# Attention with layer norm beside a quantised FFN on one core: keys and probabilities turned by DMA, context taken out in 16 blocks, queries turned in their own tile

## What is computed

```python
xn = (x - mean) / sqrt(var + 1e-5)
# attention over the HEADS of one token: 32 heads of 32 numbers
q, k, v = (xn @ W.T + b).reshape(B, S, 32, 32)     # for Wq, Wk, Wv
scores = einsum('bshd,bsgd->bshg', q, k) / sqrt(32)
scores = where(scores > 0.001, scores, -inf)
out = einsum('bshg,bsgd->bshd', softmax(scores), v)
attn = out.reshape(B, S, 1024) @ Wo.T + bo
# FFN with weights q * scale, one scale for 128 inputs
ffn = (silu(xn @ Wg.T) * (xn @ Wu.T)) @ Wd.T
return x + attn + ffn
```

## Time and profile before

| | |
|---|---|
| median of 3 runs | 2207.91 us (2207.07 to 2210.4) |
| profiled execution, its own time | 2210.67 us |
| its span | 2208.9 us |
| TensorE busy | 2100.9 us, 95% |
| VectorE busy | 1664.8 us, 75% |
| ScalarE busy | 1374.9 us, 62% |
| GpSimd busy | 1361.2 us, 62% |
| mean granted TensorE clock | 0.993 of full speed |

### The profile page before, as it was taken

The page is one execution under the profiler, slowest core; times in us unless marked ns, Lnnn a source line. Parts: engine busy times, 40 slices in busy tenths (PEclk is TensorE's granted clock), DMA queues, the critical chain, the costliest instruction groups (busy, mean ns, idle before and its releaser), DMA issues. The chain is left out here.

```text
span 2208.9 us, 39955 instructions
## 1 busy us (share of the span) xinstructions
PE 2100.9 (95%) x12032; PEld 1041.6 (47%) x12032; DVE 1664.8 (75%) x1904; ACT 1374.9 (62%) x2353; POOL 1361.2 (62%) x785
## 2 busy tenths in 40 slices
PE   7999999999999899989999999999999999999996
PEld 5555555555555554433444444444444444444444
DVE  5576667766676631049989989998998999999896
ACT  4687787887878743124565566656656665665653
POOL 1345435444445401005888888888888888888886
PEclk9999999999999999999999999999999999999998
DMA  8001000001001133412212211221221122122118
GB/s 286 30 30 40 36 28 34 32 28 47 28 28 38 68 105 113 160 34 67 57 47 52 70 44 47 66 57 47 60 64 43 47 66 57 47 66 57 43 25 309
DMA packets 156187, 144.08 MB, mean 65 GB/s; under 512 B 101488, under 2 KB 130160, under 8 KB 156144
## 3 DMA queue, kind: packets, MB, share of 16 engines
q1 hardware_dynamic: 156144, 143.50, 21.4%
HBM read 96.29 MB, written 25.17 MB: 55 GB/s over the span
## 5 line engine op out<-in xcount | busy, mean ns | idle before, releaser
L681 PE MATMUL banks<-xt,lower 128*128 128x512 f16 x3584 | 861.7, 379 | 29.9 <-ACT lower L935 16.3
L1253 POOL TENSOR_TENSOR acc<-acc,lower 128x1024 f32<-128x1024 f32 x327 | 772.1, 2365 | 176.2 <-ACT lower L962 176.2
L962 ACT ACTIVATE lower<-banks,down_scale 128x512 f32<-128x512 f32 x654 | 413.7, 683 | 356.5 <-PE banks L706 261.5
L1135 DVE SCALAR_TENSOR_TENSOR lower<-banks,gate_scale,lower 128x1024 f32<-128x1024 f32 x392 | 479.2, 1277 | 139.4 <-PE banks L681 133.5
L681 PEld LDWEIGHTS banks<-xt,lower 128*128 128x128 f16 x3584 | 337.4, 98 | 486.6 <-DVE lower L1135 80.2
L528 PE MATMUL banks<-wt,xt_tile 128*128 128x512 f16 x2304 | 552.7, 379 | 8.0 <-issue 4.1
L1135 DVE SCALAR_TENSOR_TENSOR lower<-banks,up_scale,lower 128x1024 f32<-128x1024 f32 x392 | 479.5, 1278 | 51.1 <-PE banks L681 44.9
L706 PE MATMUL banks<-lower 128*128 (+1 forms) x1792 | 459.8, 381 | 4.6 <-DMA lower<-lower 4.4
L1210 POOL TENSOR_TENSOR stacks<-unit,stacks 128x512 f16<-128x512 f32 x192 | 225.4, 1198 | 385.3 <-ACT stacks L807 385.3
L528 PEld LDWEIGHTS banks<-wt,xt_tile 128*128 (+1 forms) x2304 | 212.3, 98 | 205.0 <-issue 7.5
L706 PEld LDWEIGHTS banks<-lower 128*128 (+1 forms) x1792 | 175.7, 98 | 217.7 <-issue 18.5
(11 more groups left out here) (65 smaller groups left out, 1572.1 us busy)
## 6 DMA issues: line engine op xcount, KB each, us to landing
lower<-in_L_ffn_gate_q_dram SPq DMA_DIRECT2D x28, 512.0 KB, 3.7
lower<-in_L_ffn_up_q_dram SPq DMA_DIRECT2D x28, 512.0 KB, 4.4
lower<-in_L_ffn_down_q_dram SPq DMA_DIRECT2D x28, 512.0 KB, 3.9
x_tile<-in_L_attn_x_dram SPq DMA_DIRECT2D x16, 512.0 KB, 3.6
xt_scratch<-xt_tile SPq DMA_DIRECT2D x16, 512.0 KB, 2.7
ctx_scratch<-ctx_parts SPq DMA_DIRECT2D x16, 512.0 KB, 2.8
lower<-ctx_scratch SPq DMA_DIRECT2D x4, 2048.0 KB, 9.0
xt<-xt_scratch SPq DMA_DIRECT2D x4, 2048.0 KB, 16.3
```

The costliest lines, as they stand in the source:

```text
L681: last = mm(psum[:, 2 * (slot % 3) + c, :], gu_t[:, mat, g, :], xt[:, (2 * half + c) * CT:(2 * half + c + 1) * CT, part, g, :], start=(par ...
L962: run(down_tmp[:, buffer, c * BANK:(c + 1) * BANK], psum[:, 6 + c, :], ACT.Copy, scale=scale)\
L1135: v.scalar_tensor_tensor(out=acc_of[:, half, :], in0=gu_pair(slot % 3), scalar=scale[:, :, :].rearrange("p t k -> p (t k)")[:, bass.ds(t * ...
L1253: g.tensor_tensor(acc[:, half, ho, :], acc[:, half, ho, :], down_tmp[:, buffer, :], ALU.add).then_inc(down_added, 1)
```

## The change

Keys: SP issues one DMA transpose of 1 MB in a round, from `stacks` to `turned`, once the key units have both parts and the last scores of the tile before are made. Probabilities: four DMA transposes of 256 KB in a round, one for each eight groups, once their low part is made. TensorE keeps eight batches in a round: four of queries, now of tile i in round i (R0 to R3, steps 11 to 14), and four of values of tile i - 1 (T4 to T7, steps 4 to 7). Scores stand at steps 0 to 3, value products at 17 to 20. A group now holds tokens that lie 32 apart, so that a diagonal block of the context holds 32 neighbouring tokens. The score matmul reads the turned keys with strides, (x, r) for a fixed group g, out of [x, r, g], and its output has the order (h, r). ScalarE takes a block of the context out of PSUM straight into the high part, VectorE subtracts for the low part, 16 instructions each in a round; the reordering over partitions is left to four DMA stores of 128 KB, with runs of 1 KB. The context for the output units has runs of 32 columns in place of 128.

The core of the diff ("..." marks what is left out):

```diff
-        STEPS = [["T0"], ["T1"], ["T2"], ["T3"], ["T4"], ["T5"], ["T6", "T7"], ["S0"], ["S1"], ["S2"],
-                 ["S3"], ["T8"], ["T9"], ["T10"], ["T11"], ["X"], [], [], [], ["T12"], ["T13", "V0"],
-                 ["T14", "V1"], ["T15", "V2"], ["V3"]]
+        STEPS = [["S0"], ["S1"], ["S2"], ["S3"], ["T4"], ["T5"], ["T6"], ["T7"], [], ["X"], [], ["R0"], ["R1"],
+                 ["R2"], ["R3"], [], [], ["V0"], ["V1"], ["V2"], ["V3"], [], [], []]
-        STATS_AT, ROOT_AT, NORM_AT, SHIFT_AT, EXP_AT, MASK_AT, DIVIDE_AT, P_AT = 6, 8, 9, 10, 11, 12, 13, 15
-        CONTEXT_AT = 2
+        STATS_AT, ROOT_AT, NORM_AT, SHIFT_AT, EXP_AT, MASK_AT, DIVIDE_AT, P_AT = 0, 2, 2, 3, 4, 5, 6, 8
...
+        def block_of(k, r):
+            src = pair(v_pair(k)).rearrange("p (g r a b) -> p r b a g", r=TG, a=KT, b=TG)
+            return src[r * DH:(r + 1) * DH, r, :, :, :]
+        def context_block(k, r, part):
+            return ctx_parts[r * DH:(r + 1) * DH, :, part, :, 8 * k:8 * k + 8]
+        k_turns = turned[:, K, :].rearrange("p (x r g) -> p x r g", r=TG, g=GROUPS)
...
             def scores(j, k):
                 if k == 0:
+                    pe.wait_ge(batch_out[0], j * 4 + 2)
+                    pe.wait_ge(batch_out[1], j * 4 + 2)
+                    pe.wait_ge(k_turned, j * 16 + 16)
+                    wait_pos(pe, ctx_lo, j * 4)
                 elif k >= 2:
                     pe.wait_ge(s_out, j * 4 + (k - 1))
                 for n in range(8):
                     at = (8 * k + n) * P
                     last = mm(pair(s_pair(k))[:, n * P:(n + 1) * P], turned[:, Q, at:at + P],
-                              turned[:, K, at:at + P], start=True, stop=True)
+                              k_turns[:, :, :, 8 * k + n], start=True, stop=True)
...
             def head_products(j, k):
...
-                    pe.wait_ge(pv_out[0], j * 4 + (k - 1))
-                    pe.wait_ge(pv_out[1], j * 4 + (k - 1))
-                pe.wait_ge(batch_out[k % 2], j * 8 + (6 + k // 2 + 1))
+                    pe.wait_ge(ctx_lo, j * 4 + (k - 1))
+                pe.wait_ge(p_turned[k], j * 16 + 16)
...
+            def first_tile():
+                opening(weights, lambda: turn_x(0), first_quarter, lambda: None, lambda: turn_x(1))
+                for m in range(4):
+                    batch(0, m)
...
+            def head_products_hi(j, k):
                 act.wait_ge(pv_done, j * 4 + (k + 1))
                 if k == 0:
+                    wait_pos(act, ctx_stored, j * 64)
+                for r in range(TG):
+                    last = run(context_block(k, r, HI), block_of(k, r), ACT.Copy)
+                last.then_inc(ctx_hi, 1)
...
+            def head_products_lo(j, k):
+                dve.wait_ge(ctx_hi, j * 4 + (k + 1))
+                for r in range(TG):
+                    last = v.tensor_tensor(context_block(k, r, LO), block_of(k, r), context_block(k, r, HI),
+                                           ALU.subtract)
+                last.then_inc(ctx_lo, 1)
...
+            def turn_k(i):
+                if isinstance(i, int) and i == 0:
+                    sp.wait_ge(w_turned, 3 * KT)
+                sp.wait_ge(unit_lo, i * 6 + (2 * K + 2))
+                anchor(sp)
+                wait_pos(sp, s_done, i * 4)
+                anchor(sp)
+                sp.dma_start_transpose(turned[:, K, :].rearrange("p (x t) -> p x t", t=P), stacks[:, K, :, :].rearrange("p x c -> p (x c)"))\
+                    .then_inc(k_turned, 16)
+            def turn_probs(j, q):
+                sp.wait_ge(p_lo, j * 4 + (q + 1))
+                if q == 0:
+                    anchor(sp)
+                    wait_pos(sp, pv_done, j * 4)
+                anchor(sp)
+                at = slice(8 * q, 8 * q + 8)
+                sp.dma_start_transpose(probs_t[:, :].rearrange("p (g c) -> p g c", c=P)[:, at, :],
+                                       p_stack[:, at, :, :].rearrange("p g n h -> p (g n h)"))\
+                    .then_inc(p_turned[q], 16)
...
             def tile_2(i):
                 if not isinstance(i, int) or i + 1 < TT:
                     load_x(i + 1)
-                    store_xt(i + 1)
+                if not isinstance(i, int) or i > 1:
+                    store_context(i - 2)
                 if not projects(i):
                     for n in range(2, KT):
                         load_wo(n)
+                for q in range(4):
+                    turn_probs(i - 1, q)
+                if not isinstance(i, int) or i + 1 < TT:
+                    store_xt(i + 1)
+                if projects(i):
+                    turn_k(i)
...
                     load_wo(0)
                     load_wo(1)
-                    sp.wait_ge(ctx_stored, 16 * 2 * CT)
+                    sp.wait_ge(ctx_stored, 64 * 2 * CT)
                     load_context(0)
-                store_context(i - 1)
```

More of the change, by code:

```diff
@@ L165, in build @@
         unit_lo = sem("unit_lo")
+        k_turned = sem("k_turned")
+        p_turned = [sem(f"p_turned{k}") for k in range(4)]
         batch_done = sem("batch_done")
@@ L534, in batch @@
             def batch(j, m):
[L536 to L541, removed]
+                mat = batch_matrix(m)
+                if m % 4 == 0:
+                    pe.wait_ge(unit_lo, j * 6 + (2 * mat + 2))
+                wait_pos(pe, batch_out[m % 2], j * 4 + m // 2)
                 for n in range(8):
-                    x = 8 * (m % 4) + n
-                    src = stacks[:, m // 4, x, :] if m < 12 else p_stack[:, x, :, :].rearrange("p a b -> p (a b)")
-                    last = turn(batch_bank(m)[:, n * P:(n + 1) * P], src, ident16[:])
+                    last = turn(batch_bank(m)[:, n * P:(n + 1) * P], stacks[:, mat, 8 * (m % 4) + n, :], ident16[:])
                 last.then_inc(batch_done, 1)
@@ L644, in tile_2 @@
                             turn_x(i + 1)
+                        elif kind == "R":
+                            batch(i, n)
                         elif kind == "T":
@@ L650, in tile_2 @@
                             head_products(i - 1, n)
-            walk(pe, lambda: opening(weights, lambda: turn_x(0), first_quarter, lambda: None,
-                             lambda: turn_x(1)), tile_2)
+            def first_tile():
+                opening(weights, lambda: turn_x(0), first_quarter, lambda: None, lambda: turn_x(1))
+                for m in range(4):
+                    batch(0, m)
+            walk(pe, first_tile, tile_2)
             for n in range(LAST_UNITS, 4 * KT):
@@ L868, in tile_2 @@
                 for s in range(QUARTERS):
-                    if s == CONTEXT_AT and not (isinstance(i, int) and i == 1):
-                        context_hi(i - 2)
                     if not projects(i):
@@ L878, in tile_2 @@
                             x_part(i + 1)
+                        elif kind == "R" and n % 2 == 0:
+                            batch_copy(i, n)
                         elif kind == "T" and n % 2 == 0:
@@ L893, in tile_2 @@
                         unit_part(i, s // 4)
-                if not projects(i):
-                    context_hi(i - 1)
             root(0)
@@ L904, in first_quarter, with first_tile @@
                     unit_part(0, 5)
-            walk(act, lambda: opening(weights, lambda: x_part(0), first_quarter, lambda: root(1),
-                              lambda: x_part(1)), tile_2)
+            def first_tile():
+                opening(weights, lambda: x_part(0), first_quarter, lambda: root(1), lambda: x_part(1))
+                batch_copy(0, 0)
+                batch_copy(0, 2)
+            walk(act, first_tile, tile_2)
             def conv(mat, t):
@@ L1088, in tile_2 @@
                             x_part(i + 1)
+                        elif kind == "R" and n % 2:
+                            batch_copy(i, n)
                         elif kind == "T" and n % 2:
@@ L1118, in next_norm, with first_tile @@
                 layer_norm(1)
-            walk(dve, lambda: opening(weights, lambda: x_part(0), first_quarter, next_norm,
-                              lambda: x_part(1)), tile_2)
+            def first_tile():
+                opening(weights, lambda: x_part(0), first_quarter, next_norm, lambda: x_part(1))
+                batch_copy(0, 1)
+                batch_copy(0, 3)
+            walk(dve, first_tile, tile_2)
             dve.wait_ge(scales_loaded, 3 * 16)
```

97 lines of the change are left out of this document (43 added, 54 removed).

## The result

The changed kernel takes 2220.1 us (median of 5 runs, 2218.9 to 2222.0), the kernel before 2208.7 in the same comparison: a ratio of 1.0052, interval 1.0037 to 1.0067. It is slower by half a per cent, clear of the noise, where 2188 was forecast. The profiled execution took 2221.6 us, with a span of 2219.8.

What follows compares the result with a forecast made beforehand. TensorE, busy 95%, was taken as the bound. Fifteen rounds of 44.8 us instead of 46.1 gave -19.9, the first tile +4, the last -6: -22 us from 2210.7 or the median 2207.9, so 2188, range 2168 to 2216.

Steps and rivals of the forecast that it cites:

- the strided read: Score matmul's read of the turned keys: a group would take 0.78 us instead of 0.44, making the period 44.8 us.
- The bound from rows: High end for a strided score group: 0.88 us, the time of eight float32 transposes of x.
- Rival (d): At the score matmuls: a column costs four, groups of 1.78 us, total 2239 us; chance 0.08.
- the sign: At the score matmuls: groups taking over 1.3 us would show the forecast wrong.
- Rival (c): At the keys' DMA: 1 MB lands in 12.4 us, scores wait 2.0 a round, total 2219 us; chance 0.10.
- The ratio: VectorE's copies from PSUM, 1.22 us strided against 0.69 contiguous, used to price a score group at 0.78.
- The walk: One tile's new order followed through the engines, first with score groups of 0.44 us: a round of 43.9 us.
- R0's wait: TensorE at the first query batch: a new wait of 2.7 us for a unit copied out behind the softmax.
- DMA: Key transpose of 1 MB: lands in 8.05 us, between 6.9 and 12.4, hidden with 2.4 us to spare.
- Once-only parts: Outside the repeated rounds: +4 us for the first tile's query batches, -6 us around the last tile.
- Rival (b): TensorE's clock falls in each round, costing 1.7 us each, total 2214 us; chance 0.13.
- (a): At the score matmuls: the strided read is free, rounds of 43.9 us, total 2175 us; chance 0.17.

Runs made afterwards that it cites:

- e1: The changed kernel with the score matmul streaming 128 neighbouring keys instead of the strided view, right pairing of keys left out: 2176.6 us.
- e9: The changed kernel with a second key transpose of 768 KB, into a spare tile, issued ahead of the real one each round: 2242.3 us.
- e8: The changed kernel with groups of four neighbouring tokens, R0 to R3 at steps 13 to 16, x at 12, V0 and V1 at 16 and 17: 2114.0 us.
- e3: The changed kernel with a different shape of key read for each of the four score groups, right keys left out: 2178.3 us.
- e5: The changed kernel with groups of four neighbouring tokens instead of tokens 32 apart, so keys are read in runs of four: 2173.7 us.
- e10: The changed kernel with the score matmul's operands exchanged: strided keys stationary, contiguous queries streamed, right order of scores left out: 2175.8 us.

## Why the prediction was wrong

- **The step that failed is the strided read.** It was priced at 0.78 a group, by the ratio of two of VectorE's copies; it costs 1.72. The 15 rounds took 703.4 us, where 15 x 44.8 = 672 was forecast; those 31 us are nearly all of the miss of 32. The bound from rows, 0.88 from the float32 transposes, wasn't a bound on a stride either. Rival (d), at 1.78, was this case, with a chance of 0.08, and its 2239 lay outside the range. The prediction named the sign itself: score groups over 1.3 us. Rival (c) had a nearer time, 2219, by coincidence: the keys it put late landed with 2.7 us to spare.
- **The ratio was one engine's.** ScalarE makes copies of the same two forms, strided and contiguous, in nearly the same time, 1019 ns and 1023:

```profile
L813 ACT ACTIVATE probs_t<-banks 128x1024 f16<-128x1024 f16 x28 | 28.7, 1023 | 6.1 <-PE banks L545 5.8
```

- **The walk was right up to R0.** With 1.72 in place of 0.44 it puts the end of the fourth output at 4 x 3.02 + 0.17 + 1.54 = 13.8, 3.7 later, and R0 at 23.4 + 3.7 = 27.1. In the trace the tile's first group is at 401.93 (403.23 less 1.30): the output ends at 415.83, 13.9, and R0 starts at 27.1. R0's wait is 1.78, not 2.7, because the slower groups hold up TensorE by 5.1 (less the 0.7 at T6 that falls away) and the chain by 3.7 only, and 0.16 of the gap is the tail.
- **The period of (d)** would have been 47.8, and was 46.8. R0 comes when the chain is done, so the wait at T6 has no part in this. Some 0.2 is the chain (3.7, not 3.9), some 0.3 is V2 and V3 (0.6 with the tail, where 0.85 was given; VectorE's low part takes 1.71 for four, not 1.9), and the loop's end costs nothing where about 0.5 was carried over from the earlier trace rows.
- **DMA**: keys land in 6.7 us, below even the low end of 6.9, where 8.05 was taken. They were hidden, as said. Each 256 KB beyond the first takes 1.1 us (6.7 less 3.3, by 3), not 1.65.
- **Once-only parts**: the four query batches and their wait take 3.9 us (70.41 to 74.35), as forecast; the opening grew by 2.9 because what stands ahead of them ended 1.1 earlier than before, a point that differs between the traces (70.4, 70.9, 71.8 and 72.0 in the changed kernel, e1, e9 and e8). The last tile gave 1.9, where -6 and about +5 for (d) make -1; in e1, with the read free, it gave 4.7. The context's short runs cost next to nothing (383 ns a matmul, 381 before).
- **Rival (b)**, the clock: not in the loop of this kernel, where R0 waits 1.78, but in its last round with a projection; in e1, with 2.31, in 10 rounds. Its price of 1.7 us a fall was right. With the read free, (a) gave 2175 and e1 took 2176.6, and that agreement is luck: loop rounds without a fall are shorter than (a) had them (43.4, not 43.9), and the falls took back more than that.

The expected gain was there, 32 us with the read contiguous, and the read took 44.

## What to carry to other kernels

Before a layout is turned by DMA, look at who reads the result and in what order. Here a streamed operand of TensorE ran at full speed with four 16-bit elements in each 16 bytes, and regrouping (neighbouring tokens) removed the cost of the read without a price elsewhere; exchanging the operands nearly removed it too, but the turned order of the scores was left unused. A price for such a read has to come from a matmul that makes it: two score groups in a small test would have settled the largest term of the sum.

When work is taken off the bounding engine, walk the lists of the others again: the next wait stood on an engine's order (a unit's copy behind the softmax's division), and moving seven entries of the table by one to three steps gave 60 us (2173.7 to 2114.0), more than all the rest of the change with the read mended.

A wait on TensorE can cost more than its own length, since the clock may fall behind it, for another 1.7 us here. No length was shown to be safe: the changed kernel's loop had waits of 1.78 without a fall, while e9 had falls behind 0.85 and 0.93.

## What was not expected of the hardware

- A streamed 16-bit operand with every element in another 16-byte line costs 1.68 ns an element, four columns' time; a step of 4 bytes is nearly free (0.47 a group), and the same pattern as a weight load costs 149 ns instead of 98.
- After waits of 2.31 to 2.44 us at R0 the granted clock fell in 38 of 56 rounds (e1, e3, e5 and e10), and in the loop of the changed kernel after none of 1.78. The length of the wait doesn't explain it alone: equal waits went both ways, and e9's falls came behind 0.85, 0.93 and 1.69. What decides stays open.
- A DMA transpose of 1 MB holds the SP queue 4.8 us and lands in 6.7, while 256 KB take 1.25 and 3.3: 768 KB more cost 3.4 to 3.6.
